# One program block for the mixture and the last layer, with a counted hand-over of the shared buffers

## The chip, the cores and the metric

The kernel runs on one core of a Trainium2 chip. The metric is the device time of one launch in microseconds (us). A core has five engines with a program each: PE (matrix multiplications), DVE (vector), ACT (activations and copies), POOL (GpSimd) and SP (it only issues DMAs here). They run apart from one another and meet at semaphores. DMAs are issued by SP, ACT and POOL; those by POOL include the indirect ones, which gather or scatter rows by a list of indices in SBUF.

## The reference

1024 tokens of width 256 pass through two layers, each an attention-like part and a mixture of experts, with a residual sum behind each of the four parts. The change touches the seam between part two (the mixture of 64 experts) and part three (a linear attention):

```python
x = x + _L0_attn_ref(_layernorm(x, axis=-1), ...)
x = x + _L0_ffn_ref(_layernorm(x, axis=-1), ...)    # 64 experts, 8 per token
x = x + _L1_attn_ref(_layernorm(x, axis=-1), ...)   # cumsum of phi_k * v along the sequence
x = x + _L1_ffn_ref(_layernorm(x, axis=-1), ...)    # 8 experts, 2 per token
...
# _L0_ffn_ref
g = jnp.einsum('ecd,efd->ecf', xbuf, w_gate)
u = jnp.einsum('ecd,efd->ecf', xbuf, w_up)
y = jnp.einsum('ecf,edf->ecd', jax.nn.silu(g) * u, w_down)
y_pair = y[e_sorted, safe_pos] * (s_sorted * valid)[:, None]
out = jnp.zeros((N, D), dtype=x.dtype).at[tok_sorted].add(y_pair)
```

## The kernel before

The program has three blocks. In each every engine gets a stream of instructions, and a block ends when all five engines have met at a barrier. Block one (the program's lines up to 1259) is the first attention and half of the routing. Block two (L1333 to L1598) is the mixture of 64 experts; block three (L1690 to L2133) is the linear attention, the routing of the second mixture and its 23 tiles of expert work.

**Block two.** Per expert of 256 slots: SP loads the rows (`xg`, L1550) and, for two experts at a time, the weights; PE turns the rows (L1359), multiplies them with gate and up (L1366), turns the gated product (L1374) and multiplies it with down (L1383); ACT copies and applies silu; DVE multiplies (L1467) and copies the result out (L1459) into `yb`, from where SP stores it to `expert_outputs` in HBM (L1554, semaphores `s_st`, four of them in turn).

**What a token gets back** are 8 rows of `expert_outputs`, one for each of its 8 experts. They come by 64 gathers of POOL, each for one tile of 128 tokens and one rank k, into 16 buffers `gb`. Gathers 0 to 15 (L1537, k = 0 and 1 for the 8 tiles of tokens) stand in block two; they start once the stores of all experts but the last ones have landed, since the routing sorts the experts of a token and these gathers read only the lower part of the outputs. Gathers 16 to 63 (L2103) stand in block three. Gather g writes buffer g mod 16, so it waits until addition g - 16 is done (`s_acc0`). DVE adds each gathered row times its weight to the residual `X` (L1935, `add_gathered`), 64 additions, all in block three.

**Block three, start.** DVE writes two small tiles (`region`, `nbias`: L2019, L2020), does additions 0 to 27, and norms the first quarter of the tokens (L128 to L136; two of the eight tiles, that is why 16 + 12 additions are needed). From there a chain runs over the four quarters: PE turns (L1726) and projects (L1738), ACT makes the features (L1870 to L1876), DVE forms the running sums (L1946 to L1953), PE the output (L1751), while DVE does the next quarter's additions between those steps. Then the second mixture's routing, POOL's scatters (L2118), and 23 tiles of expert work on PE (L1811, L1820).

**Memory.** The tiles of block two and of block three that are private to a block lie at the same SBUF addresses (an `ExitStack` each); `gb`, `X`, `w8`, `ig`, the weights of the linear attention and the second mixture's weights lie outside of both. The PSUM tensors `scores` and `misc` are used by all.

## Time and profile before

| what | value |
|---|---|
| time, median of 3 runs | 994.95 us (990.76 to 996.68) |
| the profiled execution's own time | 989.93 us |
| span of its core | 988.2 us |
| mean granted TensorE clock | 0.85 of full speed |
| busy share of PE, DVE, ACT, POOL | 71%, 55%, 32%, 25% |
| first instruction of block three | 720.51 us into the span |
| start of the tiles of the second mixture | about 841 us into the span |

The span is the time from the first to the last instruction that the profiler recorded; positions below are in us from its start. A row of the timeline gives start, duration, engine, line, operation, output<-input, how many instructions are merged in the row, and in brackets how long the engine had been idle before it and what released it. "issue" as a releaser means that nothing the profile shows was waited for. Records of PE's and POOL's own queues are marked PEq and POOLq; DMA issues on SP are marked SPq.

### The profile page before, as it was taken

Reading aid. Unit: us, or ns where it says so; the run is one execution under the profiler, and the core shown is the slowest. Engines: PE = TensorE matmul, PEld = TensorE weight load, DVE = VectorE, ACT = ScalarE, POOL = GpSimd, SP = SyncE. Lnnn points to the kernel's source line nnn. Section 1 sums busy time; section 2 is a strip of 40 time slices with the busy share of each in tenths; the row PEclk is TensorE's granted clock in tenths of the full one; section 3 lists DMA queues with packets and bytes.
Section 4 is the critical chain, followed back from the end, with each engine's and each line's share of the span. In section 5 each row is a group of like instructions: output and inputs, shape, how many; then the busy total and the mean of one; then the engine's idle time right before and its main releaser. Section 6 shows DMA issues by size and latency. Waiting matters only on the chain. (4 is left out here: it accounts for less than half of the span.)

```text
span 988.2 us, 17565 instructions
## 1 busy us (share of the span) xinstructions
PE 700.7 (71%) x6542; PEld 562.0 (57%) x6587; DVE 547.2 (55%) x1652; ACT 313.0 (32%) x535; POOL 246.7 (25%) x258
## 2 busy tenths in 40 slices
PE   4957367758776787785227999999505651799995
PEld 2533255437444544763226999999504541799994
DVE  5996887599589949536601333333246784122221
ACT  1005142544454154552112444444203551111110
POOL 6003010230102020104775000000667705032322
PEclk9998877979897999579568999999856875799998
DMA  4891000640514083602966988888523306688760
GB/s 139 129 143 50 1 2 12 195 65 4 142 64 66 2 342 141 265 22 70 325 216 205 323 299 285 294 291 291 172 62 102 94 1 226 207 249 229 241 175 1
DMA packets 75561, 151.72 MB, mean 154 GB/s; under 512 B 12769, under 2 KB 36065, under 8 KB 72545
## 3 DMA queue, kind: packets, MB, share of 16 engines
q1 hardware_dynamic: 62064, 124.27, 41.3%
q0 software_dynamic: 10224, 21.12, 7.7%
q10 hardware_dynamic: 3200, 5.38, 1.5%
q8 instruction: 44, 0.72, 0.3%
q14 instruction: 29, 0.23, 0.1%
HBM read 91.01 MB, written 60.43 MB: 153 GB/s over the span
## 5 line engine op out<-in xcount | busy, mean ns | idle before, releaser
L1366 PE MATMUL scores<-wgu,zero 128*128 128x192 f32 x512 | 97.4, 335 | 0.0
L749 DVE TENSOR_REDUCE block_maxima<-scores 128x10 f32<-128x1280 f32 x64 | 92.3, 1485 | 8.1 <-PE scores L399 7.1
L1031 ACT ACTIVATE E<-scores 128x1280 f32<-128x1280 f32 x64 | 77.4, 1237 | 60.8 <-PE scores L410 32.4
L1467 DVE TENSOR_TENSOR gated_up<-gated,scores 128x192 f32<-128x192 f32 x64 | 22.7, 354 | 121.3 <-ACT gated L1508 121.3
L1811 PE MATMUL scores<-xgT,w 128*128 128x128 f32 x736 | 87.9, 279 | 0.0
L1811 PEld LDWEIGHTS scores<-xgT,w 128*128 128x128 f32 x736 | 86.1, 196 | 0.1
L1366 PEld LDWEIGHTS scores<-wgu,zero 128*128 128x128 f32 x512 | 85.2, 197 | 0.1
L1169 POOL TENSOR_SCALAR_AFFINE_SELECT E<-E 128x256 f32<-128x256 f32 x64 | 27.1, 447 | 208.4 <-ACT E L1031 208.3
L1499 ACT COPY zero<-misc 128x512 f32<-128x512 f32 x64 | 37.5, 585 | 99.5 <-PE misc L1359 99.5
L1383 PE MATMUL scores<-wd,gated_turned 96*128 96x256 f32 x256 | 66.0, 380 | 0.5 <-ACT gated_turned L1495 0.5
L1359 PE MATMUL misc<-cf,xg 128*128 128x128 f32 x256 | 40.4, 281 | 35.0 <-DMA xg<-expert_rows 35.0
L2126 POOL DMA_INDIRECT out<-yb,add_to x23 | 35.8, 1557 | 110.4 <-DVE yb L2075 108.4
L2088 DVE TENSOR_TENSOR cum<-low,scores 128x512 f32<-128x512 f32 x23 | 15.8, 686 | 77.4 <-issue 67.9
L1459 DVE COPY xnT<-scores 128x512 f32<-128x512 f32 x64 | 44.2, 691 | 24.5 <-PE scores L1383 24.5
L1359 PEld LDWEIGHTS misc<-cf,xg 128*128 128x128 f32 x256 | 32.4, 144 | 43.4 <-issue 22.1
L2103 POOL DMA_INDIRECT gb<-expert_outputs,gather_slots x48 | 51.2, 1067 | 21.7 <-issue 11.9
L1537 POOL DMA_INDIRECT gb<-expert_outputs,gather_slots x16 | 15.3, 955 | 162.9 <-DMA expert_outputs<-xnT 158.3
L399 PE MATMUL scores<-cb 128*128 128x128 bf16 x256 | 54.2, 233 | 1.9 <-issue 0.9
L824 DVE TENSOR_TENSOR tmp<-Y,LB 128x120 f32<-128x120 f32 (+35 forms) x244 | 50.1, 245 | 0.3
L833 DVE TENSOR_TENSOR Y<-Y,tmp 128x120 f32<-128x120 f32 (+35 forms) x244 | 50.0, 245 | 0.1
L199 POOL DMA_INDIRECT expert_rows<-stack_q,scatter_slots x32 | 31.4, 980 | 64.5 <-issue 61.7
L464 PE MATMUL misc<-LB,E 32*32 32x32 f32 x512 | 17.6, 231 | 40.5 <-DVE LB L839 32.5
(295 smaller groups left out, 1513.9 us busy)
## 6 DMA issues: line engine op xcount, KB each, us to landing
w<-in_w SPq DMA_DIRECT2D x23, 1024.0 KB, 5.0
expert_rows<-zero SPq DMA_DIRECT2D x32, 512.0 KB, 6.3
xg<-expert_rows SPq DMA_DIRECT2D x64, 256.0 KB, 3.4
expert_outputs<-xnT SPq DMA_DIRECT2D x64, 256.0 KB, 3.1
wgu<-in_wgu SPq DMA_DIRECT2D x32, 384.0 KB, 3.7
rows_by_expert<-zero SPq DMA_DIRECT2D x21, 408.0 KB, 6.0
wd<-in_wd SPq DMA_DIRECT2D x32, 192.0 KB, 4.1
w<-in_w ACTq DMA_DIRECT2D x8, 512.0 KB, 10.9
```

Of the source, the lines that this page charges most:

```text
L399: ins = nc.tensor.matmul(scores[:, slot, o + w - P:o + w], identb, mask[c, it], start=False, stop=True)
L749: nc.vector.tensor_reduce(bm[:, c, h, :], scores[:, slot, 0:WIDE].rearrange("p (a n) -> p a n", n=P), AX.X, ALU.max).then_inc(s_fd, 1)
L824: nc.vector.tensor_tensor(part, Yc[:, x, 0:n, k:k + 1].to_broadcast([P, n, w]), LB[:, k:k + 1, k + 1:SB].to_broadcast([P, n, w]), ALU.mult ...
L833: nc.vector.tensor_tensor(below, below, part, ALU.add).then_inc(s_inv, 1)
L1031: nc.scalar.activation(to[:, h, :], scores[:, k % 2, 0:WIDE], ACT.Exp, scale=SCALE).then_inc(s_fa, 1)
L1359: ins = nc.tensor.transpose(misc[:, j % 2, c:c + P], xg[:, j, t, k * P:(k + 1) * P], identf)
L1366: ins = nc.tensor.matmul(scores[:, j % 2, t * 2 * F0:(t + 1) * 2 * F0], xgT[:, j % 2, k, t * P:(t + 1) * P], wgu[:, j // GE, j % GE, k, :] ...
L1383: ins = nc.tensor.matmul(scores[:, j % 2, 1024 + t * D:1024 + (t + 1) * D], hT[:, j % 2, t * P:(t + 1) * P], wd[:, j // GE, j % GE, :], st ...
L1459: nc.vector.tensor_copy(yb[:, j % NY].rearrange("p t d -> p (t d)"), scores[:, j % 2, 1024:1536]).then_inc(s_yv, 1)
L1499: nc.scalar.copy(xgT[:, j % 2].rearrange("p k n -> p (k n)"), misc[:, j % 2, :]).then_inc(s_xt0, 1)
L1811: ins = nc.tensor.matmul(scores[:, j, c:c + P], w13[:, q, k, c:c + P], xgT[:, j, k, :], start=(k == 0), stop=(k == KT - 1))
L2103: pool.indirect_dma_start(out=gb[:, g % NG, :], out_offset=None, in_=ybuf, in_offset=bass.IndirectOffsetOnAxis(ap=ig[:, t, k:k + 1], axis= ...
```

## The change

Blocks two and three become one. The code of block two moves into five functions (`tensor_mixture` and so on), which block three's engine functions call first. In place of the barrier stands a semaphore `s_left`: PE, DVE, ACT and SP each raise it by one when they have finished with the mixture, and every engine waits for four before it touches memory that the two parts share. POOL does not raise it. Two things stand ahead of the wait: DVE's additions 0 to 15, which in the block before came behind the two small writes, and POOL's gathers 16 to 63. Before gather 16 POOL waits for all stores of expert outputs. The semaphore `s_w8`, for which nothing waited, goes.

```diff
+        s_left = sem("mixture_left")
...
-            with nc.Block() as block:
-                @block.tensor
-                def _(pe):
+                def tensor_mixture(pe):
...
+                    pe.wait_ge(s_y0, E0)
+                    nc.tensor.sem_inc(s_left, 1)
...
-                    nc.vector.sem_inc(s_w8, 1)
...
+                    dve.wait_ge(s_yv, E0)
+                    nc.vector.sem_inc(s_left, 1)
...
+                    act.wait_ge(s_hc0, E0)
+                    nc.scalar.sem_inc(s_left, 1)
...
+                    for y in range(NY):
+                        pool.wait_ge(s_st[y], 16 * (E0 // NY))
...
                     for j in range(NY):
                         sp.wait_ge(s_st[j], 16 * (E0 // NY))
+                    nc.sync.sem_inc(s_left, 1)
...
                 with nc.Block() as block:
                     @block.sync
                     def _(sp):
+                        sync_mixture(sp)
+                        sp.wait_ge(s_left, 4)
                         sp.dma_start(gate1[:], ...)
...
+                        tensor_mixture(pe)
+                        pe.wait_ge(s_left, 4)
...
+                        scalar_mixture(act)
+                        act.wait_ge(s_left, 4)
...
+                        vector_mixture(dve)
...
+                        for g in range(NG):
+                            add_gathered(g)
+                        dve.wait_ge(s_left, 4)
                         dve.wait_ge(s_lw, 16 * 8)
                         link(nc.vector.tensor_scalar(region[:], iota8, float(N), -1.0, ALU.mult, ALU.add))
                         nc.vector.tensor_scalar(nbias[:], bias[:], -1.0, None, ALU.mult).then_inc(s_nb, 1)
-                    for g in range(NG):
-                        add_gathered(g)
                         gathered(0, 0, GQ)
                         norm_lin(0)
...
+                        gpsimd_mixture(pool)
                         for g in range(NG, NT * K0):
                             t, k = gather_at(g)
                             pool.wait_ge(s_acc0, g - NG + 1)
...
+                        pool.wait_ge(s_left, 4)
                         nc.gpsimd.memset(rows1[:, :, :, D:RW], 0.0).then_inc(s_tok, 1)
```

How the instructions stand on the two engines that meet at the seam. On POOL before, with the last gathers of block two (L1537), the jumps at the barrier (L1333, L2096), and the first of block three (L2103); `row_added` is `s_acc0`, `down_done` is `s_y0`:

```order
L1537 DMA gb<-expert_outputs,gather_slots 128x256
L1537 DMA gb<-expert_outputs,gather_slots 128x256 [waits down_done]
L1333 UNCONDITIONAL_BRANCH
L2096 UNCONDITIONAL_BRANCH [waits barrier_Pool_Activation_PE_DVE_SP_gather]
L2103 DMA gb<-expert_outputs,gather_slots 128x256 [waits row_added]
L2103 DMA gb<-expert_outputs,gather_slots 128x256 [waits down_done,row_added]
```

The same place on POOL in the change; `y_stored0` to `y_stored3` are the four `s_st`:

```order
L1541 DMA gb<-expert_outputs,gather_slots 128x256
L1541 DMA gb<-expert_outputs,gather_slots 128x256 [waits down_done]
L2121 DMA gb<-expert_outputs,gather_slots 128x256 [waits y_stored3,y_stored2,row_added,y_stored1,y_stored0]
L2121 DMA gb<-expert_outputs,gather_slots 128x256 [waits down_done,row_added]
L2121 DMA gb<-expert_outputs,gather_slots 128x256 [waits row_added]
```

Gather 16 now follows gather 15 directly, behind the stores and the first addition; no barrier and no jump stands between them.

On DVE before, from the last copies of the mixture's results (L1459) over the barrier to the first additions (L1935; `rows_moved` are the landings of the gathers):

```order
L1459 COPY xnT<-scores 128x512 [waits y_stored3,down_done]
L1333 UNCONDITIONAL_BRANCH
L1927 UNCONDITIONAL_BRANCH [waits barrier_Pool_Activation_PE_DVE_SP_release]
L2019 TENSOR_SCALAR region<-cf 128x8 [waits lin_weights]
L2020 TENSOR_SCALAR minus_bias<-bias_lin 128x6 [waits chain1]
L1935 SCALAR_TENSOR_TENSOR X<-gb,w,X 128x256 [waits rows_moved0]
L1935 SCALAR_TENSOR_TENSOR X<-gb,w,X 128x256 [waits rows_moved1]
```

And in the change, with additions 0, 15 and 16:

```order
L1461 COPY xnT<-scores 128x512 [waits y_stored3,down_done]
L1951 SCALAR_TENSOR_TENSOR X<-gb,w,X 128x256 [waits down_copied,rows_moved0]
...
L1951 SCALAR_TENSOR_TENSOR X<-gb,w,X 128x256 [waits row_added,rows_moved15]
L2038 TENSOR_SCALAR region<-cf 128x8 [waits lin_weights,mixture_left]
L2039 TENSOR_SCALAR minus_bias<-bias_lin 128x6 [waits chain1]
L1951 SCALAR_TENSOR_TENSOR X<-gb,w,X 128x256 [waits row_added,rows_moved0]
```

The first sixteen additions have moved ahead of the wait for the other engines; the two small writes stand behind them, and behind `mixture_left`.

## Rows read from the trace of the kernel before

**Rows 1.** The page: the chain that ended last, its largest shares by line
```profile
PE scores L1811 9%; PE misc L1820 4%; POOL rows_by_expert L2118 1%; PE scores L1751 1%; PE scores L1738 1%; POOL gb L2103 1%; DMA rows_by_expert<-rows_ffn,slots 1%; PE misc L1803 1%; DVE cum L1951 1%; DVE relu L1946 1%; DVE X L1935 0%; DMA xn_lin<-rows_by_expert 0%; DVE kv L1947 0%; PE misc L1726 0%; ACT xnT L1858 0%
```
**Rows 2.** Timeline from the end of the mixture to the barrier
```profile
694.33 0.99 POOL L1537 DMA_INDIRECT gb<-expert_outputs,gather_slots  x1 [158.31 <-DMA expert_outputs<-xnT]
...
706.57 0.69 DVE L1459 COPY xnT<-scores 128x512 f32<-128x512 f32 x1 [1.12 <-PE scores L1383]
706.95 0.95 POOL L1537 DMA_INDIRECT gb<-expert_outputs,gather_slots  x1 [0.30 <-issue]
708.20 0.95 POOL L1537 DMA_INDIRECT gb<-expert_outputs,gather_slots  x1 [0.30 <-issue]
...
713.23 0.95 POOL L1537 DMA_INDIRECT gb<-expert_outputs,gather_slots  x1 [0.30 <-issue]
```
**Rows 3.** Timeline behind the barrier: additions 0 to 17, gathers 16 to 20
```profile
720.51 0.39 SPq L1693 DMA_DIRECT2D gate<-in_gate  x1
720.55 0.17 DVE L2019 TENSOR_SCALAR region<-cf 128x8 f32<-128x8 f32 x1 [13.29 <-PEq L1333]
720.76 0.17 DVE L2020 TENSOR_SCALAR minus_bias<-bias_lin 128x6 f32<-128x6 f32 x1
720.84 7.21 DVE L1935 SCALAR_TENSOR_TENSOR X<-gb,w,X 128x256 f32<-128x256 f32 x18
721.58 0.95 POOL L2103 DMA_INDIRECT gb<-expert_outputs,gather_slots  x1 [7.40 <-DVE X L1935]
722.84 1.28 POOL L2103 DMA_INDIRECT gb<-expert_outputs,gather_slots  x1 [0.30 <-DVE X L1935]
724.42 4.45 POOL L2103 DMA_INDIRECT gb<-expert_outputs,gather_slots  x1 [0.30 <-DVE X L1935]
729.17 0.95 POOL L2103 DMA_INDIRECT gb<-expert_outputs,gather_slots  x1 [0.30 <-issue]
```
**Rows 4.** Timeline: gather 27, addition 27, the first norm, the first projection
```profile
739.23 0.95 POOL L2103 DMA_INDIRECT gb<-expert_outputs,gather_slots  x1 [0.30 <-issue]
742.02 0.49 DVE L1935 SCALAR_TENSOR_TENSOR X<-gb,w,X 128x256 f32<-128x256 f32 x1 [0.81 <-DMA gb<-expert_outputs,gather_slots]
742.54 0.75 DVE L128 BATCH_NORM_STATS2 stats<-X 128x6 f32<-128x256 f32 x2
```
**Rows 5.** Waits from 745.8 to 762: engine line <- releaser: us in total, times, longest
```profile
PE misc L1726 <- DVE xn_lin L136: 39.9, 1, 39.9
ACT low L1870 <- PE scores L1738: 3.9, 2, 3.5
DVE relu L1946 <- ACT relu L1876: 2.6, 1, 2.6
DVE X L1935 <- DMA gb<-expert_outputs,gather_slots: 2.6, 3, 1.1
```
**Rows 6.** Line L1537 and line L2103 of all gathers: instructions, then us from issue to landing
```profile
L1537 POOL DMA_INDIRECT gb<-expert_outputs,gather_slots x16: 949/953/992, 694.3 to 713.2; - x16
...
DMA to landing us min/median/max: 2.7/3.1/4.4
...
L2103 POOL DMA_INDIRECT gb<-expert_outputs,gather_slots x48: 949/953/4447, 721.6 to 786.2; - x48
...
DMA to landing us min/median/max: 2.7/2.8/6.2
```
**Rows 7.** Line L1554, the last stores of expert outputs: durations in ns, span, landing
```profile
L1554 SPq DMA_DIRECT2D expert_outputs<-xnT x8: 332/333/343, 690.9 to 707.3; - x8
...
DMA to landing us min/median/max: 2.1/2.8/3.5
```
**Rows 8.** Timeline at 774 and at 748: gathers under single DVE operations
```profile
748.04 0.88 DVE L1935 SCALAR_TENSOR_TENSOR X<-gb,w,X 128x256 f32<-128x256 f32 x2
748.14 1.21 POOL L2103 DMA_INDIRECT gb<-expert_outputs,gather_slots  x1 [0.30 <-issue]
...
773.84 0.69 DVE L1946 TENSOR_TENSOR relu<-relu,low 128x512 f32<-128x512 f32 x1 [2.67 <-ACT relu L1876]
774.10 1.26 POOL L2103 DMA_INDIRECT gb<-expert_outputs,gather_slots  x1 [0.31 <-issue]
```
**Rows 9.** The chain that ended last from 742: the projections of quarters 0 and 2
```profile
748.23 4.99 PE scores L1738 x12
...
784.66 2.86 PE scores L1738 x12
```
**Rows 10.** Windows: us, busy us (x instructions) of PE, PEld, DVE, ACT, POOL, clock, DMA share, GB/s
```profile
706.00:712.00 6.00, 0.53 (x3) 0.13 (x1) 0.69 (x1) 0.00 (x0) 4.48 (x6) 0.68 0.73 217
712.00:720.00 8.00, 0.00 (x0) 0.00 (x0) 0.00 (x0) 0.00 (x0) 1.88 (x2) 0.50 0.17 50
...
746.00:750.00 4.00, 2.85 (x8) 2.21 (x9) 3.28 (x8) 2.07 (x3) 3.08 (x4) 0.50 0.33 90
```

1037 lines of the change are left out of this document (519 added, 518 removed).

## The prediction

> **What bounds the kernel now.** I read the page's chain of work that ended last first, to see whether the seam lies on it at all. Most of it is PE's expert work of the second mixture (L1811, L1820), but POOL's gathers (L2103), the additions (L1935) and the running sums (L1951) stand in it too [rows 1]: the end of the kernel hangs on that tail, the tail on the linear attention, and that on the gathers. A microsecond won at the seam should therefore come out at the end, unless something between holds a fixed date. Then I read the timeline over the seam. DVE ends its last copy of the mixture at 706.57 + 0.69 = 707.26. POOL is then in the middle of its first sixteen gathers, which started at 694.33 and follow one another every (713.23 - 708.20) / 4 = 1.26 us; number 15 runs from 713.23 to 714.18 [rows 2]. Then nothing runs on any engine until 720.51, and DVE had been idle for 13.29 us, released by the barrier (L1333) [rows 3]. So the barrier is open 6.3 us after POOL's last instruction.
>
> Behind the barrier DVE does 18 additions back to back in 7.21 us, one every (7.21 - 0.48) / 17 = 0.396 us, from 720.84 to 728.05. Gather 16 starts at 721.58, gather 17 takes 1.28 and gather 18 takes 4.45 us instead of 0.95, and gather 19 starts at 729.17 [rows 3]. At the pace of 1.26, number 19 would have started at 721.58 + 3.77 = 725.35; so 3.8 us went to these two gathers. Gather 18 ends at 728.87, 0.82 behind the last addition of the run: it stood still while the additions ran. From gather 19 to 27 the pace is (739.23 - 729.17) / 8 = 1.26 again; addition 27 starts at 742.02, 2.79 behind its gather's start, and the first norm follows at 742.54 [rows 4]. So the first norm, with which the linear attention starts, is dated by POOL alone: start of gather 16, plus 11 gathers, plus a landing.
>
> From there the gathers no longer set the date. Between 745.8 and 762 the additions wait 2.6 us for them in three pieces while the long waits are PE's for DVE and ACT's for PE; the steps of the quarter hang on one another [rows 5]. The distance of gathers 28 to 63 to the first norm does not change either, as they follow at the same pace. So I let the whole shift of the first norm go through to the end.
>
> **The change part by part.** *The barrier on POOL's way goes.* Gather 16 stands behind gather 15, the stores and addition 0. The last store is issued at 707.3 and takes at most 3.5 us to land, so by 710.8 or so [rows 7]. Addition 0 needs DVE's last copy (707.26) and gather 0, which started at 694.33 and landed within 4.4 us [rows 2, 6]. Both are earlier than gather 15's end, so gather 16 starts at 713.23 + 1.26 = 714.49 instead of 721.58: 7.1 us. The added waits on the stores cost nothing under this cover; it is 3.4 us thick, and a store that landed later than 714.2 would be paid in full.
>
> *The run of additions leaves gathers 17 and 18.* In the change only additions that follow a landing stand beside gathers 16 to 27, one every 1.26 us as from 730 on, where the gathers take 0.95. The 3.8 us go. Together 7.1 + 3.8 = 10.9 us: addition 27 at 731.1.
>
> *The additions 0 to 15 now run beside gathers 11 to 15.* This is the only new cost. After its last copy DVE starts at about 707.4. Gather g lands at about 694.33 + 1.26 g + 3.1 [rows 2, 6], addition g is due at 707.4 + 0.396 g; these cross at g = 12 (712.5 against 712.2). So 12 additions run back to back until about 712.2, and 13 to 15 follow their landings, the last at about 716.4. Four gathers (11 to 14, from 708.20 to 712.9) can be hit. From below the cost is 0: gather 16 in the old run took 0.95 [rows 3]. From above, gather 11 stands still until 712.2 + 0.82 = 713.0 where it would have ended at 709.15: 3.9 us. The nearest row is the old run itself, which starts 0.74 us ahead of its first gather, as here 0.8 us ahead of gather 11. Its pattern (first gather free, second +0.33, third held to the run's end plus 0.82) gives gather 12 +0.33 and puts gather 13, from 711.04, to 713.0 instead of 711.99: +1.0 more. I take 1.4 us.
>
> A second row shows that a gather normally loses only what is left of one addition: the gather at 748.14 takes 1.21 while the first of two additions, from 748.04, ends at about 748.5, and it does not wait for the second; the one at 774.10 takes 1.26 under an operation of 0.69 that reads two SBUF tiles [rows 8]. By this, four gathers lose at most 0.48 each, 1.9 in all. The Trainium skill has this rule (SBUF — State Buffer, Who interferes with whom): a DVE instruction with two SBUF inputs and a GpSimd instruction that reads SBUF exclude one another, and the second waits for the first to end. The trace agrees in the rows at 748 and 774; the 4.45 us of gather 18 is longer than any one instruction and more than the page's rule explains. It speaks against moving the additions here; by it alone the time would be 994.95 - (10.9 - 1.9) = 985.95, an estimate from that page's rule.
>
> *The other additions of the change are covered.* `region` and `nbias` (0.17 each) now come behind addition 15 at about 716.9, and addition 16 is due only at 714.49 + 2.8 = 717.3; if they came late, ACT and PE would wait for them only at the first norm. SP's two loads for block three start when its own stores have landed, at about 711 instead of 720.51 [rows 3]. The four increments are in by then: PE and ACT stop before DVE's last copy, SP is the last at about 711. The wait for four, behind which DVE's small writes stand, is over before addition 15. Nothing inside the mixture changes.
>
> *The clock of TensorE.* PE does almost nothing from 706 on, and the granted clock is at 0.50, its lower level of 1.2 GHz, from 712 until beyond 750 [rows 10]. The gap gets 9 to 11 us shorter but stays long, so PE should start cold again: the first projection of twelve matmuls took 4.99 us where a later one took 2.86 [rows 9]. I cost this at nothing, and take the difference, 2.1 us, as what the place of the clock's rise can give or take over the four quarters.
>
> **Sum.** 7.1 + 3.8 - 1.4 = 9.5 us. Against the profiled execution, 989.93 becomes 980.4 (a span of 978.7). That execution lies 5.0 us under the median of the runs shown, whose extremes are 5.9 us apart; a shift does not depend on this, so the median becomes 994.95 - 9.5 = 985.4 us. One per cent is 9.95 us, about what a measurement of this kernel can tell from no change: the forecast stands right beside this bound.
>
> **Rivals.** *The long stall comes back* (chance 0.22). If the state of gather 18, held to the end of a run, takes gather 11, or if it is something of POOL's own queue that strikes once behind a pause of additions, 3.8 to 3.9 us stay: 10.9 - 3.9 = 7.0, so 988. For it: two of the three gathers in the old run were hit. Against it: the run is 12 long instead of 18, and in rows 8 the wait ended with one instruction.
>
> *POOL's pause is its own* (0.12). The 6.3 us between gather 15's end and the opening of the barrier could be POOL finishing its indirect transfers, and it could need that time before gather 16 with or without a barrier. Then gather 16 starts at about 720.5; it wins 1.1 there, and the 3.8, since the additions are done: 4.9 us, so 990. Against it: all 48 gathers of L2103 ran through, with a median of 953 ns [rows 6] and no such pause.
>
> *Slower* (0.04). Without the barrier POOL issues 54 scatters, 16 and 48 gathers in one go, 118 where it had at most 87 in a block (48, 16 and 23 in block three). If what held gather 18 for 3.5 us is want of room in its queue, it would come back for later gathers. A loss is measured only from 10.9 + 9.95 = 20.9 us on, that is from six such holds; then the time is about 1005. Against it: 87 went through in block three with one long hold, and that one ended with the additions.
>
> **How the numbers follow.** The forecast case (0, 1.4 or 1.9 us of collision) has 0.60: 984.05 to 985.95, and with the clock's 2.1 either way 982 to 988. The rest, 0.02, is a hidden date further down. The range reaches from 980, the free case with the clock in favour and 2 us of scatter of a median, to 991, the pause case with 1 us: it leaves out the slower case and tails of the others. Faster by over 1% is below 985.0: about half of the forecast case, and a small part of the long stall by scatter, 0.40. Slower 0.05, the rest 0.55.
>
> **What would show it.** Right, if gather 16 starts 1.26 us behind gather 15, at about 714.5 plus the collision; if gathers 16 to 18 take 0.95; if addition 27 starts at 731 to 735; and if the distance from there to the end of the span stays at 988.2 - 742.0 = 246.2 within 2 us. The collision is the sum of what gathers 11 to 15 take over 0.95. Wrong, if POOL idles several us between gathers 15 and 16 (the pause case), if one of gathers 11 to 14 ends at 713 and had started at 708 to 710 (the long stall), if the 246 us grow (a hidden date, or the clock), or if the mixture ahead of 706 runs differently.

## The result, and the profile after

| | kernel before | changed kernel |
|---|---|---|
| time, median | 992.86 us (988.85 to 996.68, 6 runs) | 980.67 us (976.02 to 984.36, 6 runs) |
| the profiled execution's own time | 989.93 us | 984.08 us |
| span | 988.2 us | 982.4 us |
| mean granted TensorE clock | 0.85 | 0.84 |

The ratio of the times is 0.9881, with a 95% interval of 0.9847 to 0.9916: 12.2 us or 1.2% less. The whole interval lies under 1, so the kernel became faster; it reaches to a gain of 0.8% (8.3 us), so that the gain is over the 1% of the prediction is likely and not certain. The forecast was 985.4 in a range of 980 to 991; 980.67 lies just inside its lower end. Of all runs here one, of kernel f3, took 1038.04 us at a granted clock of 0.75 where the others of f3 had 0.85 to 0.86; it is in no ratio below.

The timeline of the changed kernel over the seam, the lines that answer to [rows 2] and [rows 3]. A row gives start, duration, engine, line, operation, count and, in brackets, the idle time before it and its releaser. L1541 are gathers 0 to 15 (the first one shown is 11), L2121 the gathers from 16 on, L1951 the additions, L1461 the mixture's last copy:

```profile
706.41 0.69 DVE L1461 COPY xnT<-scores 128x512 f32<-128x512 f32 x1 [1.12 <-PE scores L1385]
707.24 5.23 DVE L1951 SCALAR_TENSOR_TENSOR X<-gb,w,X 128x256 f32<-128x256 f32 x13
707.25 0.95 POOL L1541 DMA_INDIRECT gb<-expert_outputs,gather_slots  x1 [0.30 <-issue]
708.51 1.24 POOL L1541 DMA_INDIRECT gb<-expert_outputs,gather_slots  x1 [0.30 <-issue]
710.05 3.26 POOL L1541 DMA_INDIRECT gb<-expert_outputs,gather_slots  x1 [0.30 <-issue]
710.68 0.39 SPq L1704 DMA_DIRECT2D gate<-in_gate  x1
...
714.86 0.95 POOL L1541 DMA_INDIRECT gb<-expert_outputs,gather_slots  x1 [0.31 <-issue]
715.17 0.48 DVE L1951 SCALAR_TENSOR_TENSOR X<-gb,w,X 128x256 f32<-128x256 f32 x1 [2.70 <-DMA gb<-expert_outputs,gather_slots]
716.12 0.95 POOL L2121 DMA_INDIRECT gb<-expert_outputs,gather_slots  x1 [0.30 <-issue]
...
718.14 0.18 DVE L2038 TENSOR_SCALAR region<-cf 128x8 f32<-128x8 f32 x1
...
729.96 0.95 POOL L2121 DMA_INDIRECT gb<-expert_outputs,gather_slots  x1 [0.30 <-issue]
...
732.79 0.48 DVE L1951 SCALAR_TENSOR_TENSOR X<-gb,w,X 128x256 f32<-128x256 f32 x1 [0.88 <-DMA gb<-expert_outputs,gather_slots]
733.31 0.75 DVE L128 BATCH_NORM_STATS2 stats<-X 128x6 f32<-128x256 f32 x2
```

The mixture ends when it did: the last copy at 707.10 against 707.26 [rows 2]. Gather 16 starts at 716.12, 1.26 behind gather 15, with POOL idle for 0.30 as between any two gathers; before, it was 8.35 behind [rows 2, 3]. From gather 16 to 27 it takes (729.96 - 716.12) / 11 = 1.26 each, and no gather is held there. What is new is the third row of POOL, gather 13: it takes 3.26 us and ends at 713.31, 0.83 behind the end of the run of thirteen additions (707.24 + 5.23, about 712.48). Gather 12 takes 1.24. Together gathers 11 to 15 take 2.6 us more than 0.95 each. The first norm starts at 733.31 instead of 742.54 [rows 4], 9.2 us earlier.

In this profiled execution part of that is lost again. The chain that ended last, from 735 on: twelve of the 24 matmuls of the projection in quarters 0, 1 and 2 (start, us, what), to be read against 4.99 and 2.86 in [rows 9]:

```profile
739.02 5.50 PE scores L1751 x12
758.15 4.84 PE scores L1751 x12
778.53 4.89 PE scores L1751 x12
```

The windows over the same stretch say why. Columns are the window, its length, busy us (x instructions) of PE, PEld, DVE, ACT and POOL, the granted clock, DMA share and GB/s:

```profile
745.00:752.00 7.00, 2.47 (x11) 1.77 (x10) 4.96 (x10) 5.41 (x12) 5.39 (x6) 0.99 0.34 101
752.00:762.00 10.00, 8.48 (x21) 6.54 (x22) 8.99 (x27) 2.66 (x5) 7.64 (x8) 0.50 0.35 96
762.00:769.00 7.00, 4.82 (x28) 4.20 (x27) 2.28 (x5) 5.45 (x13) 5.30 (x6) 0.99 0.38 110
769.00:782.00 13.00, 8.11 (x20) 6.23 (x21) 11.89 (x33) 3.98 (x7) 8.26 (x10) 0.50 0.28 81
```

In this stretch TensorE is at its higher level of 2.4 GHz only from 745 to 752 and from 762 to 769, and the projections of quarters 1 and 2 begin at 1.2 GHz. From addition 27 to the last matmul of the kernel it took 240.8 us where the kernel before took 235.2: 5.7 us more.

The end of the kernel moved too, by something that the prediction had not seen. POOL's last scatter, in the kernel before:

```profile
979.27 1.55 POOL L2126 DMA_INDIRECT out<-yb,add_to  x1 [2.00 <-DMA out<-yb,add_to]
```

and in the changed kernel:

```profile
975.70 1.55 POOL L2145 DMA_INDIRECT out<-yb,add_to  x1 [2.01 <-DMA out<-yb,add_to]
```

Before, the span ends at 988.21, 7.39 us behind the end of this row; in the changed kernel at 982.36, 5.10 us behind it. The records of POOL's own queue show one instruction in that gap, POOL's drain at the end of the block: it took 8.93 us before and 6.65 us after, counted from 0.2 us ahead of the scatter. So 2.3 us of the gain lie behind the last piece of work.

The span thus goes: 9.2 us from the seam, 2.3 us from the tail, minus 5.7 us behind addition 27, most of it the clock's, gives 5.8, which is 988.2 - 982.4. The medians show 12.2. The times of either kernel fall in two groups: 988.85, 990.76, 990.76 and 994.95, 995.86, 996.68 before; 976.02, 976.59, 977.35 and 984.00, 984.08, 984.36 after. The profile of the kernel before (989.93) matches its lower group and that of the changed kernel (984.08) is one of its upper group, so the 5.8 us set a short execution before against a long one after. Lower group against lower group it is 14.2 us, upper against upper 11.8. In the changed kernel the mean granted clock is 0.854 to 0.856 in the lower group and 0.843 to 0.848 in the upper one; that the clock's places make the groups fits this, but no execution near 976 was profiled.

### The profile page after: what moved, and what is told of

The parts are those of the page before. It is cut to its first block, busy times and chain, and to the rows that moved or that the text cites. A ratio compares the mean times of both kernels' runs of the same rounds, so it can differ in the third digit from the quotient of the medians.

```text
span 982.4 us, 17604 instructions
## 1 busy us (share of the span) xinstructions
PE 713.3 (73%) x6586; PEld 566.7 (58%) x6587; DVE 548.0 (56%) x1652; ACT 313.0 (32%) x535; POOL 245.7 (25%) x258
## 4 chain that ended last, share of the span: by engine, by line
PE 33%; POOL 8%; issue 4%; DVE 3%; DMA 2%; ACT 1%; POOLq 0%; SPq 0%; DVEq 0%; ACTq 0%
PE scores L1824 9%; PE scores L1368 8%; PE scores L1385 5%; POOL expert_rows L199 5%; PE misc L1833 4%; PE misc L1361 3%; PE scores L1751 2%; POOL rows_by_expert L2137 1%; PE scores L1376 1%; PE scores L1764 1%; POOL gb L2121 1%; DMA rows_by_expert<-rows_ffn,slots 1%; DVE X L1951 1%; PE misc L1816 1%; DVE cum L1967 1%
## 5 line engine op out<-in xcount | busy, mean ns | idle before, releaser
L1541 POOL DMA_INDIRECT gb<-expert_outputs,gather_slots x16 | 17.8, 1115 | 162.2 <-DMA expert_outputs<-xnT 157.6
L1461 DVE COPY xnT<-scores 128x512 f32<-128x512 f32 x64 | 44.2, 691 | 24.2 <-PE scores L1385 24.2
L2121 POOL DMA_INDIRECT gb<-expert_outputs,gather_slots x48 | 48.1, 1003 | 14.6 <-issue 12.2
```

The costliest lines, as they stand in the source:

```text
L1461: nc.vector.tensor_copy(yb[:, j % NY].rearrange("p t d -> p (t d)"), scores[:, j % 2, 1024:1536]).then_inc(s_yv, 1)
L2121: pool.indirect_dma_start(out=gb[:, g % NG, :], out_offset=None, in_=ybuf, in_offset=bass.IndirectOffsetOnAxis(ap=ig[:, t, k:k + 1], axis= ...
```

## The experiments

Twelve runs of eight kernels were made in three series, each series on one chip with its own runs of the kernel before. In the first series the kernel before took some 1055 us, and all kernels ran at that level. In the other two it took 991 us, near the result above. The record gives chip number 9 for the first and the third series and 12 for the second, so the number of the chip does not tell the two levels apart.

One table for all, read from the profiled execution of each. "Gathers 0 to 27" is the distance of their starts; at 1.257 us a piece, undisturbed, it is 33.95. "Held" is what gathers 11 to 15, and 16 to 27, take over 0.95 us each. "Addition 27" is its start in the span, "27 to last matmul" runs from there to the end of PE's last matmul, and "tail" from the end of POOL's last scatter to the end of the span.

| kernel | gathers 0 to 27 | held 11-15 | held 16-27 | addition 27 | 27 to last matmul | tail | span |
|---|---|---|---|---|---|---|---|
| before | 44.90 | 0 | 3.81 | 742.0 | 235.2 | 7.39 | 988.2 |
| before again (f1) | 44.89 | 0 | 3.81 | 741.4 | 234.8 | 7.39 | 987.2 |
| changed | 36.56 | 2.58 | 0 | 732.8 | 240.8 | 5.10 | 982.4 |
| changed again (f2) | 36.47 | 2.47 | 0 | 734.8 | 235.9 | 5.10 | 979.3 |
| gaps (f3) | 34.11 | 0.14 | 0 | 733.7 | 237.2 | 5.10 | 979.5 |
| PE kept busy (f4) | 35.64 | 1.65 | 0 | 734.0 | 237.8 | 5.10 | 980.6 |
| barrier kept, additions ahead (g1) | 41.00 | 0.32 | 0 | 737.6 | 235.0 | 7.39 | 983.7 |
| no barrier, additions behind (g2) | 37.69 | 0.28 | 3.41 | 735.7 | 235.3 | 5.10 | 979.8 |
| gather 16 delayed (g3) | 44.23 | 2.20 | 0 | 743.9 | 234.2 | 5.10 | 986.9 |
| extra block (g4) | 34.35 | 0.37 | 0 | 733.9 | 234.6 | 5.10 | 977.3 |
| first series: changed (e1) | 46.25 | 0 | 3.20 | 775.9 | 262.6 | 5.10 | 1047.2 |
| first series: additions behind (e2) | 47.94 | 0 | 4.17 | 777.5 | 261.3 | 5.10 | 1047.6 |
| first series: gaps (e3) | 46.16 | 0 | 0.28 | 774.5 | 264.4 | 5.10 | 1047.7 |
| first series: gather 16 delayed (e5) | 52.72 | 0 | 0 | 782.9 | 266.9 | 5.10 | 1058.5 |

The column of addition 27 also holds what went on ahead of the seam. The mixture's last copy ends at 707.3 to 707.5 in f1 and g1, and at 708.3 to 710.6 in f2, f3, f4, g2, g3 and g4. The difference begins in block one, which the change does not touch: PE's 21st matmul starts at 20.25 us in f1 and g1 and at 22.08 in these six. It is no property of the merged block, for the kernel before has 22.08 in its first profile, and e1, e2 and e3 have 20.33. In the result's own pair the copies end at 707.26 and 707.10. So f2 has addition 27 only 6.7 us ahead of f1, while its seam is 8.4 us shorter.

### First series

**e1, the changed kernel as it is.**

> The changed kernel once more, for a second profile and more times. In its first profile the first norm of the linear attention starts 9.2 us earlier than before (733.31 against 742.54), but the span is only 5.8 us shorter, and the three projections (12 matmuls each) took 5.50, 4.84 and 4.89 us where before they took 4.99, 2.86 and 2.86; its six times fall in two groups, about 976.7 and about 984.1. Theory 'clock places': the seam gives 9.2, and the groups come from where the granted clock stands when the projections start. Then a profile of a run near 976 has projections of about 2.9 to 3.9 us, and the distance from the first norm to the end of the span is 242 to 244 us, one near 984 has 249. Rival 'ahead of the seam': the groups differ before 707 us; then the distance is the same 249 and the last copy of the mixture (707.1) has moved by several us. Time 976 to 984, ratio to before 0.985 to 0.991.

Measured: 1051.91 us (12 runs) against 1055.47, ratio 0.9973 (0.9953 to 0.9994). The gain is 3.6 us here, not the 12 that was expected, and with 1051.91 in place of 976 to 984 the run does not answer its own question of the two groups. The timeline at the seam shows another order of events:

```profile
745.79 0.95 POOL L1541 DMA_INDIRECT gb<-expert_outputs,gather_slots  x1 [0.30 <-issue]
...
752.12 0.69 DVE L1461 COPY xnT<-scores 128x512 f32<-128x512 f32 x1 [1.88 <-PE scores L1385]
752.96 6.42 DVE L1951 SCALAR_TENSOR_TENSOR X<-gb,w,X 128x256 f32<-128x256 f32 x16
...
756.06 4.15 POOL L2121 DMA_INDIRECT gb<-expert_outputs,gather_slots  x1 [9.31 <-DVE X L1951]
```

Here gather 15 ends at 746.74, 6.1 us *before* the mixture's last copy at 752.81. So gather 16 waits for the stores and not for POOL, all sixteen additions stand ready and run in one piece, and it is now gather 16 that is held, until 760.21, 0.83 behind the end of the run at 759.38. In such an execution a barrier would stand behind the stores too, and POOL's way to it would be covered by them, so little is left of the 7.1 us. The tail is 5.10 us here too, so its 2.3 us would be the larger part of the 3.6. Both steps are argued: the kernel before was timed in this series, not profiled.

**e2, additions 0 to 15 behind the count again.**

```diff
-                        for g in range(NG):
-                            add_gathered(g)
                         dve.wait_ge(s_left, 4)
                         ...
                         nc.vector.tensor_scalar(nbias[:], bias[:], -1.0, None, ALU.mult).then_inc(s_nb, 1)
+                        for g in range(NG):
+                            add_gathered(g)
```

> One part of the change undone: one block, POOL's gathers 16 to 63 free of the wait, but additions 0 to 15 again stand behind the wait for four and the two small writes. They start when SP's last store has landed, at about 711 instead of 707.24, as one run of 16 until about 717. Theory 'run holds a gather' (a gather that starts while DVE's additions follow back to back can stand still until the run ends plus 0.83 us): two gathers from 711 on go through with up to 0.4 us more, one stands still until about 718, so addition 27 comes at 734 to 736 instead of 732.8: 1 to 3 us slower than the changed kernel. Rival 'POOL's queue' (the long gather is a matter of POOL's own queue after a fixed number of gathers): gather 13 is the long one again, by about 2.3 us, wherever the additions stand. Rival 'nothing': with the additions late no gather is long and it is 2.6 us faster. Against before: 8 to 11 us faster.

Measured: 1054.03 us, ratio 0.9991 (0.9971 to 1.0011). Addition 27 starts 1.6 us later than in e1; one gather takes 4.84 us, as the theory of the run said, and it is number 17 and not number 13, which speaks against a fixed place in POOL's queue. The time is 2.1 us above e1, within the intervals of both; the 8 to 11 us against the kernel before did not come, as in e1.

**e3, a short instruction between the additions.** If what holds a gather is DVE's unbroken run, an instruction without an SBUF input between two additions may let it through. `gap` is a new tile of 128x16.

```diff
                         for g in range(NG):
                             add_gathered(g)
+                            nc.vector.memset(gap[:, g:g + 1], 0.0)
```

> The changed kernel with one small DVE instruction (a memset of 128 x 1, which reads no SBUF tile) behind each of additions 0 to 15. Theory 'run holds a gather': the gap lets the waiting gather in, so gathers 11 to 15 take 0.95 to 1.3 us each, none 3.26, and gather 16 starts at about 714 instead of 716.1; the first norm at about 731 instead of 733.3; 2 us faster than the changed kernel, 11 us faster than before. Rival 'POOL's queue': gather 13 takes 3.3 again and the time is the changed kernel's. Rival 'only the run's length counts': the run gets longer by 12 x 0.1 us, and the held gather with it, 1 us slower.

Measured: 1048.25 us, ratio 0.9920 (0.9898 to 0.9943), which lies clear of that of e1. No gather is held: all that gathers 16 to 27 take over their 0.95 us is 0.28 in sum, where it was 3.20. From the end of the mixture's last copy to gather 27 it is 17.35 us against 20.29 in e1, 2.9 less; the table's 46.16 against 46.25 hides this, since the last copy came 1.6 us later in this execution. The two profiled executions themselves took the same (1049.38 and 1048.92), so the 3.7 us between the medians rest on the times alone.

**e5, gather 16 delayed.** Eight clearings of a tile, each waited for, stand between gather 15 and 16 on POOL.

```diff
                         gpsimd_mixture(pool)
+                        for r in range(8):
+                            nc.gpsimd.memset(zero[:], 0.0).then_inc(s_idle, 1)
+                            pool.wait_ge(s_idle, r + 1)
                         for g in range(NG, NT * K0):
```

> The changed kernel with eight memsets of 128 x 1024 on POOL between gathers 15 and 16, each about 1.0 us (0.96 in block one), so gather 16 starts about 8.5 us later, at 724.6, and addition 27 at about 741.3, near where it was before (742.0). Theory 'the date of the first norm carries all of the gain': the time is that of before within 2 us (ratio 0.997 to 1.002). Rival 'gain elsewhere too' (from the missing barrier for the other engines, the earlier loads, or the mixture itself): it stays 3 us or more faster than before though the first norm is as late.

Measured: 1057.82 us, ratio 1.0020 (1.0005 to 1.0035). Gather 16 starts 10.1 us later than in e1 and finds the additions done, so it is not held; addition 27 starts 7.0 us later, and the median is 5.9 us higher than in e1, and 2.4 over the kernel before. What is lost at gather 16 comes out at the end.

### Second series

**f1, the kernel before, unchanged**, and **f2, the changed kernel, unchanged**, to have a second profile of both.

> The kernel before, unchanged, for a profile on the chip of this job. On the chip of the last job every kernel took 1048 to 1058 us, and in the profile of the changed kernel PE's results reached ACT up to 24 us after PE's recorded work in three places, the last of them in the first quarter of the linear attention; the mixture's last copy came at 752.8 and the stores after POOL's first sixteen gathers had ended (746.7), so the barrier there could cost little. Theory 'POOL last': where the chip is like the first one (about 992 us) the last gather ends 7 us behind the last copy and the barrier opens 6.3 us behind it; where it is like the second (about 1055 us) the copies and stores are last, and the barrier opens 1 to 2 us behind the last store's landing. Ratio to before 1.000.

> The changed kernel beside it. On a chip like the first: 976 to 984 us, ratio 0.985 to 0.991, first norm 9 us earlier; three projections of 2.9 to 5.5 us by where the granted clock stands, which moves the distance from addition 27 to the end of the span between 242 and 250 us. On a chip like the second: ratio 0.997, 2 to 4 us. Rival 'the gain is the same on every chip': 9 us on both.

Measured: f1 992.53 us, ratio 1.0015 (0.9989 to 1.0040); f2 980.59 us against 990.92, ratio 0.9901 (0.9871 to 0.9932). The seam repeats to a few hundredths: 44.89 and 36.47 us for gathers 0 to 27, against 44.90 and 36.56. In f1 the last gather ends at 713.58, 6.3 us behind the mixture's last copy, so POOL is last there again, as expected. The clock's places do not repeat. In the changed kernel it now rises in time for quarter 1, as the windows of f2 show (columns as above):

```profile
753.00:759.00 6.00, 4.49 (x12) 3.37 (x12) 5.46 (x16) 0.30 (x1) 4.78 (x5) 0.50 0.37 107
760.00:769.00 9.00, 6.49 (x36) 5.73 (x35) 5.81 (x15) 7.56 (x16) 6.87 (x8) 1.00 0.36 102
```

and the projections of quarters 1 and 2 take 2.86 us each again. The distance from addition 27 to the last matmul is 235.9 us, within 1.1 of the kernel before. So the 5.7 us lost in the first profile belong to that execution and not to the change. Losses of this kind are not rare: f3 below took 5.50, 4.84 and 2.86 us for the three, one quarter more at the lower level.

**f3, the gaps of e3 in this series.**

> The changed kernel with a memset of 128 x 1 behind each of additions 0 to 15, as in the last job, where no gather beside the additions took over 1.12 us while the changed kernel had one of 4.15. Theory 'run holds a gather': gathers 11 to 18 take at most 1.4 us each, addition 27 comes 2 to 3 us earlier than in the changed kernel, measured from the last copy of the mixture; 2 to 3 us faster than the changed kernel, if the clock's places allow it to be seen. Rival: a held gather of 3 us or more is there again, and the last job's was chance.

Measured: 978.05 us median of five runs, 977.6 of the four that are in the ratio, 0.9857 (0.9826 to 0.9887). The rows of POOL beside the additions of f3 (L1542 are gathers 11 to 15, L1952 additions, L2037 the gaps):

```profile
709.98 0.89 DVE L1952 SCALAR_TENSOR_TENSOR X<-gb,w,X 128x256 f32<-128x256 f32 x2
710.42 0.06 DVE L2037 MEMSET gap<- 128x1 f32 x1
710.60 1.10 POOL L1542 DMA_INDIRECT gb<-expert_outputs,gather_slots  x1 [0.30 <-issue]
...
711.20 0.48 DVE L1952 SCALAR_TENSOR_TENSOR X<-gb,w,X 128x256 f32<-128x256 f32 x1
711.23 0.06 DVE L2037 MEMSET gap<- 128x1 f32 x1
...
712.01 0.95 POOL L1542 DMA_INDIRECT gb<-expert_outputs,gather_slots  x1 [0.30 <-issue]
```

The additions come every 0.41 us instead of every 0.396, so the gaps cost DVE 0.2 us over all sixteen, and no gather is held. From the last copy to addition 27 it is 23.8 us against 26.5 in f2, 2.7 less, where 2 to 3 were expected. Whether it is the gap itself that lets a gather in, or the changed pitch that keeps gathers from starting at the wrong moment (see g4), these kernels do not tell apart: they change both. It is the fastest of all kernels here by its median, 2.5 us under f2 (3.0 with the four runs); their intervals overlap, so in this series the difference is likely rather than shown. In e3 against e1 the intervals do not touch.

**f4, PE kept busy before the first quarter.** Matmuls on unused data stand in PE's stream at the pace of additions 12 to 28 and up to the first norm, so that the clock is up when the linear attention starts.

```diff
+                        for mark, least, n in [(s_acc0, g, 5) for g in range(12, 28)] + [(s_acc0, 28, 5), (s_var, 4, 5), (s_std, 4, 2)]:
+                            pe.wait_ge(mark, least)
+                            for r in range(n):
+                                nc.tensor.matmul(misc[:, 1, r % 4 * P:(r % 4 + 1) * P], identf, identf, start=True, stop=True)
```

> The changed kernel with matmuls of 128 x 128 on PE that nobody reads, five behind each of additions 12 to 27 and a few up to the first norm, to keep PE at work until the linear attention starts. Theory 'clock places': the granted clock then is at its upper level at the first projection, which takes 2.9 us for 12 matmuls instead of 5.0 to 5.5, and addition 27 to the first scatter gets 2 us shorter or more; 1 to 4 us faster than the changed kernel. Rival 'the clock is not it': the projection stays at 5 us, or the time stays the changed kernel's. Rival 'in the way': the last of these matmuls delay PE's turn of the first quarter by up to 1 us.

Measured: 979.15 us, ratio 0.9885 (0.9850 to 0.9919), which the intervals do not part from f2; 1 to 4 us were expected. Its windows:

```profile
720.00:739.00 19.00, 18.54 (x165) 18.21 (x163) 8.53 (x22) 1.58 (x2) 14.43 (x16) 1.00 0.37 104
739.00:750.00 11.00, 5.53 (x25) 4.48 (x24) 8.04 (x16) 7.95 (x15) 8.56 (x9) 1.00 0.36 102
751.00:760.00 9.00, 8.11 (x20) 6.23 (x21) 8.03 (x26) 2.66 (x5) 6.87 (x8) 0.50 0.34 101
```

The first quarter's projection, all 24 matmuls, takes 5.45 us instead of 7.8 in f2. Then the clock falls at 750.5, after a stretch in which PE had been busy 5.53 of 11 us, and quarters 1 and 2 take 7.9 us each instead of 5.9. The chain that ended last also changes: in this stretch it now runs through the gathers, as in

```profile
738.75 3.35 DMA gb<-expert_outputs,gather_slots
...
744.83 0.30 issue
745.13 3.21 DMA gb<-expert_outputs,gather_slots
```

So a faster quarter 0 meets gathers that come at POOL's pace, and the place of the clock's rise is not a free gain.

### Third series

**g1, the barrier kept, additions 0 to 15 ahead of it.** It parts the change in two.

```diff
                     copy_down(NB - 1, E0 - 1, E0 // NY - 1)
...
+                    for g in range(NG):
+                        add_gathered(g)
...
-                    for g in range(NG):
-                        add_gathered(g)
```

> The kernel before with its barrier kept; only the additions 0 to 15 are moved ahead of it, to the end of VectorE's part of the mixture. It parts what the change did at the seam into the barrier's share and the additions' share. Theory: the run of additions holds one of the gathers 12 to 14 (2.6 us, as in the changed kernel) and gather 17 behind the barrier is no longer held (3.8 us back), so addition 27 starts about 1.2 us earlier than in the kernel before, near 740.5 to 741, all else stays, and the median is 1 to 2 us under the kernel before. Rival: the place of the additions is most of the gain and the barrier little; addition 27 would start near 735 and the time fall by 6 to 8 us. On the tail: POOL's last drain took 8.93 us in the kernel before and 6.65 in every kernel with one block less; with the block kept it should take 8.93 again, while if it was the order of the work at the seam that shortened it, 6.65.

Measured: 988.86 us against 990.79 (12 runs), ratio 0.9975 (0.9947 to 1.0003): 1.9 us under, as forecast, but not clear of no change. The timeline (L1548 gathers up to 15, L1483 the additions, L2112 gather 16):

```profile
707.41 4.44 DVE L1483 SCALAR_TENSOR_TENSOR X<-gb,w,X 128x256 f32<-128x256 f32 x11
707.70 1.01 POOL L1548 DMA_INDIRECT gb<-expert_outputs,gather_slots  x1 [0.31 <-issue]
...
710.28 1.21 POOL L1548 DMA_INDIRECT gb<-expert_outputs,gather_slots  x1 [0.31 <-issue]
...
713.05 0.95 POOL L1548 DMA_INDIRECT gb<-expert_outputs,gather_slots  x1 [0.30 <-issue]
...
721.00 0.95 POOL L2112 DMA_INDIRECT gb<-expert_outputs,gather_slots  x1 [7.00 <-POOLq L1333]
```

POOL's 7.00 us of idle time in front of gather 16 are the barrier's (7.40 in [rows 3]), and they stay. The rival, with addition 27 near 735, falls. The 3.8 us of gathers 17 and 18 are gone. What I had not expected is that the eleven additions hold nobody: gathers 11 to 15 lose 0.32 in sum, where the changed kernel lost 2.6. So addition 27 comes at 737.6 instead of 740.5 to 741, and the additions' share is 44.90 - 41.00 = 3.9 us: the 3.81 of the two gathers, plus 0.40 of a shorter pause, minus the 0.32. The tail is 7.39 us, as in the kernel before.

**g2, the additions behind the count** (the kernel of e2; the records give chip number 9 for both).

> The changed kernel with the additions 0 to 15 put back behind the count, run again on another chip than the first time. Theory: gathers 0 to 15 end near 714.2 with none held (2.6 us back), the run of additions then starts near 714 and holds gather 17 or 18 until it has ended near 721 (3.8 to 4.9 us lost), so addition 27 starts 1 to 3 us later than in the changed kernel and the time is 1 to 3 us above it, about 982. Rival: additions that stand on VectorE when gather 16 wants them cost nothing once the barrier is gone; addition 27 starts 2 us earlier and the time is near 978.

Measured: 980.26 us, ratio 0.9881 (0.9843 to 0.9918). The timeline around the run:

```profile
713.78 6.81 DVE L1951 SCALAR_TENSOR_TENSOR X<-gb,w,X 128x256 f32<-128x256 f32 x17
...
714.25 1.23 POOL L1541 DMA_INDIRECT gb<-expert_outputs,gather_slots  x1 [0.30 <-issue]
715.79 1.28 POOL L2121 DMA_INDIRECT gb<-expert_outputs,gather_slots  x1 [0.30 <-DVE X L1951]
717.37 4.05 POOL L2121 DMA_INDIRECT gb<-expert_outputs,gather_slots  x1 [0.30 <-DVE X L1951]
```

The pattern of [rows 3] is back (+0.33, then a hold to the run's end plus 0.83), worth 3.7 us in sum, but gathers 11 to 14 are free, and the difference to the changed kernel is 37.69 - 36.52 = 1.2 us at gather 27. In the time it cannot be seen: 980.26 against 980.59 for f2. The removal of the barrier alone brings 44.90 - 37.69 = 7.2 us at the seam and the tail's 2.3.

**g3, gather 16 delayed** (the kernel of e5).

> The changed kernel with eight clearings of a small tile on POOL between gather 15 and gather 16, which on the first chip moved gather 16 about 10 us later. Theory (the date of addition 27 and the last drain carry the whole difference between the two kernels): addition 27 starts near 742.5, the last drain stays at 6.65 us, and the time is 2 to 3 us under that of the kernel before, near 990. Rival (the date is given back by the clock or by a later wait): the time stays within 2 us of the changed kernel, near 981.

Measured: 989.73 us, ratio 0.9973 (0.9944 to 1.0001), and addition 27 at 743.9. The delay puts the distance of gathers 0 to 27 at 44.23, almost that of the kernel before, and the time goes back with it, except for (44.90 - 44.23) + 2.3 = 3.0 us that should be left. The ratio gives 2.7 and the medians 1.1, both inside the interval of 0 to 5.5 us; the rival's 981 is far off. So nothing behind the first norm holds a date of its own.

**g4, one more block.** It tests the tail.

```diff
+                with nc.Block() as extra:
+                    @extra.sync
+                    def _(sp):
+                        sp.wait_ge(s_w, 16)
+
                 with nc.Block() as block:
                     @block.sync
                     def _(sp):
                         sync_mixture(sp)
```

> The changed kernel with one more program block put between the first stage and the merged block; it holds a single wait of the DMA queue that is met long before. It tests the tail: POOL's last drain took 8.93 us with three blocks and 6.65 us with two. Theory A: the drain grows with the number of blocks that ran before it; it takes 8.93 us again and the time is 2 to 3 us above the changed kernel, plus what the extra block costs at its own place (1 to 5 us). Theory B: it depends on what POOL issued in its own block, and stays at 6.65 us.

Measured: 981.27 us, ratio 0.9892 (0.9843 to 0.9941); the last drain takes 6.65 us and the tail is 5.10. So the number of blocks alone does not set the drain (the extra one gave POOL nothing to do). The last drain took 8.93 us in the three profiles where the mixture was a block of its own, with its scatters and gathers 0 to 15 behind a drain of their own, and 6.65 in the eleven where POOL issued them in the same block as the end. Why stays open.

This kernel, whose seam is that of the changed one, also shows that the hold is not certain:

```profile
710.40 5.36 DVE L1956 SCALAR_TENSOR_TENSOR X<-gb,w,X 128x256 f32<-128x256 f32 x13
710.65 1.07 POOL L1541 DMA_INDIRECT gb<-expert_outputs,gather_slots  x1 [0.30 <-issue]
712.02 0.95 POOL L1541 DMA_INDIRECT gb<-expert_outputs,gather_slots  x1 [0.30 <-issue]
713.28 1.21 POOL L1541 DMA_INDIRECT gb<-expert_outputs,gather_slots  x1 [0.30 <-issue]
```

Thirteen additions in one piece, these three gathers inside them, and none delayed by more than 0.26 us. In the changed kernel the same run cost 2.6. The next table shows, from the single records of each profile, where in an addition each gather starts. Back-to-back additions start every 0.396 us, so "offset" is the time from the last addition's start to the gather's start, and "extra" is what the gather takes over 0.953 us:

| kernel | first gather: offset, extra | next | next |
|---|---|---|---|
| before | 0.351, 0.00 | 0.024, 0.33 | 0.024, **3.49** |
| changed | 0.007, 0.00 | 0.070, 0.28 | 0.026, **2.30** |
| f2 | 0.190, 0.16 | 0.029, **2.31** | |
| g3 | 0.059, 0.30 | 0.029, **1.91** | |
| f4 | 0.137, 0.21 | 0.026, 0.33 | 0.025, **1.11** |
| g2 | 0.076, 0.28 | 0.029, 0.33 | 0.030, **3.10** |
| e2 | 0.101, 0.25 | 0.027, **3.89** | |
| e1 | 0.320, **3.20** | | |
| g1 | 0.290, 0.06 | 0.025, 0.00 | 0.089, 0.26 |
| g4 | 0.248, 0.11 | 0.032, 0.00 | 0.089, 0.26 |
| f3 (gaps) | 0.206, 0.15 | 0.398, 0.00 | 0.027, 0.00 |

Three things stand in it. The short delays fill up to one moment: offset and extra add up to 0.34 to 0.36 in nearly all of them, so such a gather waits until 0.35 us into the addition, which is recorded with 0.48, and then goes. A gather that was delayed so makes the next one start 0.35 + 0.95 + 0.30 = 1.60 us behind that addition's start, which is four additions (1.58) and 0.02: the next gather always starts 0.02 to 0.03 behind an addition. And of the nine long holds (f1 repeats the kernel before), eight start at 0.024 to 0.030; only the one of e1 does not. All nine end 0.82 or 0.83 us behind the end of an addition that another does not follow at once. With 0.95 for the gather itself this too is 0.35 us into that last addition: a held gather goes at the same moment of an addition as a briefly delayed one, only not in the first that comes. A start at that offset is not enough: two gathers with it passed free (g1, g4), and in the kernel before (both profiles), f4 and g2 one each got 0.33 only. This is a pattern in the records; no run here set the offset on purpose.

## Why the prediction came out, step by step

**The barrier on POOL's way: 7.1 us forecast, 7.09 measured.** Gather 16 moved from 8.35 to 1.26 us behind gather 15. The stores and the first addition stood in no one's way, as forecast, in every profile of the second and third series in which gather 16 was not held back by the edit itself. In the first series that cover was gone, since the stores came last, and the kernel gained 3.6 us instead of about 11. The prediction named the cover of 3.4 us, for a store that lands late, but not an execution whose whole mixture ends 46 us later.

**The run of additions leaves gathers 17 and 18: 3.8 forecast, 3.81 measured** (held 16-27 in the table). g1, with the barrier kept, comes to 3.9, of which 3.81 are this part.

**The collision with gathers 11 to 14: 1.4 forecast, 2.6 and 2.5 measured in the two profiles.** Of the pattern that was carried over, the plus 0.33 and the hold to the run's end plus 0.82 were right (0.28 and 0.83), and so was the gather that it takes, number 13. The size was wrong in one input: the prediction took the run to end when its twelfth addition met its landing, near 712.2, with gather 13 from 711.04. The run began at 707.24 and ended at 712.48, and gather 13 stood at 710.05, since in this execution the gathers started 0.9 us earlier (693.40 against 694.33). So the run began 0.01 us ahead of gather 11 and not 0.8, as the prediction had it for its likeness to the old run. A hold's price is the run's end minus the gather's start, so those two dates add up in full. g1, g4 and f4 with 0.3, 0.4 and 1.7 us show that the term turns on tenths of a microsecond in where the run starts; the bounds of 0 to 3.9 hold all of them. What one execution shows for this term is thus a draw from a wide range, and that the first profile held number 13 was luck: in f2 it was 12, in f4 14. The length of the run does not decide whether a gather is held: eleven and thirteen additions passed without one.

The Trainium skill (SBUF — State Buffer, Who interferes with whom) has a DVE instruction with two SBUF inputs and a GpSimd instruction that reads SBUF exclude one another. The gathers that lose 0.06 to 0.33 us agree with that roughly: they wait within one addition, to 0.35 of its 0.48 us. Three that started 0.007, 0.025 and 0.032 us into an addition lost nothing (changed kernel, g1, g4), where by the rule they would have waited. The nine that take 2.07 to 4.84 us wait over up to ten additions and not for one, and the page's rule does not cover them.

**The other additions of the change: nothing forecast, nothing seen.** SP's first load starts at 710.68 where about 711 was said, and `region` is written at 718.14, ahead of all that needs it.

**Sum at the seam: 9.5 forecast; 44.90 - 36.56 = 8.3 measured** between gathers 0 and 27, and 9.2 at the first norm, because this mixture's gathers started 0.9 us earlier. The second pair of profiles gives 44.89 - 36.47 = 8.4.

**The tail: not forecast, 2.3 us.** The prediction took the distance from addition 27 to the end as one piece of 246.2 us that stays. It went over the fact that the end of the last block is itself a piece of the change: two barriers became one, and the drain in front of the last one is not the same. A row could have warned of it: 7.4 us lie behind the last scatter. This is the term that the prediction left out. It more than makes up for the collision that was sized too small: 9.5 forecast against 8.4 + 2.3 = 10.7 by the rows. The median of f2 lies 10.3 us under the kernel before of its series, that of the result 12.2, with an interval of 8.3 to 15.2. So two misses of opposite sign, 1.2 and 2.3 us, are both smaller than what the times can tell, and the total speaks for the 7.1 and the 3.8 and for neither of these two. Of the 4.7 us by which 980.67 lies under the forecast, 2.1 come from the base: the forecast started from 994.95, the median of three runs, and with all six it was 992.86.

**The clock: nothing forecast, 2.1 either way.** On average the middle was right to about 1 us: f2, f3, g2, g3 and g4 need 235.9, 237.2, 235.3, 234.2 and 234.6 us from addition 27 to the last matmul, the kernels with the barrier 235.2, 234.8 and 235.0. The width was too small, for one profile of the changed kernel lost 5.7. The 2.1 us were the difference for one quarter's projection. In that profile three projections took 5.50 + 4.84 + 4.89 = 15.2 us where [rows 9] has one at 4.99 and the later ones at 2.86: 4.5 us, so the same 2 us were paid in two more quarters. By the prediction's own sign, 246.2 us to the end within 2, this profile falls outside (249.6: 5.7 for the clock, less 2.3 of the tail), while f2 has 244.6.

**The rivals.** *POOL's pause is its own* falls: where gather 15 came last and nothing was put behind it (changed kernel, f2, f3, f4, g2, g4), gather 16 follows after 0.30 us, and with the barrier (g1) the pause is there whatever the additions do. So the 6.3 us belong to the drain and the barrier. *Slower by want of room in the queue* falls: of the 48 gathers in one go behind 70 other issues, the longest took 1.84 us:

```profile
L2121 POOL DMA_INDIRECT gb<-expert_outputs,gather_slots x48: 949/953/1840, 716.1 to 777.6; - x48
```

*A hidden date* falls with e5 and g3. *The long stall comes back* was half right: it came back, one gather earlier or later by execution, but it cost 2.3 and not 3.9 us, since its gather was already 2.8 us into the run.

## What to carry to other kernels

When a barrier is removed, look for what stood on the engine that arrives last, and cost only that: 13.29 us of idle time on DVE were worth 7.1 at the seam, because POOL ended late and needed the drain. Look at both ends of the block, for the drain at the far end changes as well. And where a run of two-input DVE instructions meets POOL's gathers, expect a cost between nothing and the whole rest of the run, and try a cheap instruction without an input between them; here it cost 0.2 us of DVE's time, and its median was 3.7 us lower in the first series and 2.5 in the second, where the intervals overlap.

## What the runs showed of the hardware that was not expected

- A run of back-to-back additions can hold one gather until the run ends (2.07 to 4.84 us for 0.95; the end comes 0.82 or 0.83 behind the run, nine times of nine), and another run of the same length lets all gathers pass with 0.26 at most. The hold ends where a short delay ends, 0.35 us into an addition. Eight of the nine started 0.02 to 0.03 us behind an addition's start, and a delayed gather puts the next one just there. With a 128x1 memset between the additions none was held, in two series.
- POOL's drain ended 1.9 us behind its last scatter at the end of block one, 5.8 us behind its last gather in the block of the mixture, 7.2 us behind the last scatter in the kernel before, and 4.9 in the changed one. What sets it stays open; the number of blocks is not it (g4).
- The same program took some 1055 us in one series and 991 in the others, with the same chip number in the first and the third. In e1 DVE and ACT waited for something that the profile can only call "remote" in a few places, up to 8.0 us at once before the seam (the waits below), and the mixture's last copy came 46 us later than in the changed kernel's profile. The waits of e1 from 640 to 755, us in total, times, longest:

```profile
POOL gb L1541 <- DMA expert_outputs<-xnT: 172.9, 1, 172.9
...
ACT gated L1511 <- remote: 8.0, 1, 8.0
...
DVE xnT L1461 <- remote: 6.4, 2, 4.2
```

In that series the change is worth 0.3% and not 1.2%: what a change at a seam brings depends on which engine ends last there, and that is not a property of the program alone.
